# The columns of a group stored half by half: every TensorE read becomes one run of words

## The chip, the core and the metric

The kernel runs on one core of one Trainium2 chip. A core has TensorE (matrix products), VectorE (DVE), ScalarE (ACT), GpSimd (POOL), SyncE (SP, which issues the transfers), an on-chip memory SBUF of 128 partitions and a smaller memory PSUM into which TensorE writes. The metric is the device time of one execution in microseconds (us). Before the change the median of three runs is 1070.05 us (1069.75 to 1071.53).

## The reference

`x` has 128 batches, 64 heads and 1024 positions. Two layers are added onto it in turn.

```python
# layer 0: a base weight and a low-rank adapter, picked per batch by its id
y  = einsum('bsd,od->bso', x, W) + bias          # d = o = 1024
h  = einsum('bsd,brd->bsr', x, A[ids])           # rank 16
x1 = x + y + einsum('bsr,bor->bso', h, B[ids])
# layer 1: a causal convolution of each head with a filter K of 1024 taps
out = x1 + mask * (irfft(rfft(x1, 2048) * rfft(K, 2048))[..., :1024] + x1 * D)
```

K is a sum over 64 complex exponentials for each head, and mask cuts each batch at its own length.

## The kernel before, in words

All is computed in float32 by splitting: a number is the sum of a high part in the type fp32r and a low part, and a product of two numbers becomes three matmuls (high by high, low weights by high, high weights by low). ScalarE makes a high part by a copy (line 687), VectorE the low part by a subtraction (line 1105).

**First stage (to about 769 us).** The 128 batches are cut into 16 groups of 8. The data of a group are [128 positions, 8 tiles, 512 columns], where a column is one (head, batch) pair: 64 heads by 8 batches. The eight batches are two halves of four, so a head has eight words in a row: four of half 0, then four of half 1. The product of the 1024 by 1024 weight with the group is done by Strassen's scheme in Winograd's form: seven products of half-sized blocks in the place of eight, separately for the even output tiles (p = 0) and the odd ones (p = 1). A block holds the columns of one half only. So the moving operand of such a matmul is 256 columns in 64 runs of 4 words, 8 words apart. `block` (line 300) and `half` (line 304) cut these views. Four sums T1 to T4 of blocks are made by VectorE (lines 1209 to 1226); T1 to T3 are stored with the slot between head and batch. Their high part `t_hi` has two slots, so its runs of 4 words lie 8 words apart; their low part `t_lo` has three, so its runs lie 12 words apart. T4 is kept in the place of `x_lo`; its high and low parts go to `t_hi` and `t_lo` like the others.

`product_hi` (line 1810) runs 16 matmuls over a high moving part, high and low weights in turn; `product_lo` (line 1816) runs 8 over a low moving part with the high weights. `adapters_down` (line 1738) computes h with 32 matmuls a group, `adapters_up` (line 1782) adds the adapters' product; both read halves. Each matmul loads its own 128 by 128 weights first. The even tiles of group 0 alone are computed without the scheme, from all 512 columns at once (line 1748), with their adapters on line 1774.

TensorE's order is written out by hand: for each group and for both p the products P1, then `adapters_down`, P2, P6, the adapters of block 11, P3, P7, block 12, then P5, P4, blocks 22 and 21. Between them ScalarE copies one PSUM bank onto another (`seed_b`, `seed_c`, `seed_e`, on line 687), and ScalarE and VectorE carry results to `x1_sb` (lines 690 and 1262), which is laid out by head, tile and batch. From there they go to a scratch tensor in DRAM.

**Second stage (from about 769 us).** Head by head, 30 products on line 1970 of 384 or 512 columns, and two rotations of a state on line 2005 with 128 columns. Its moving operands of 512 columns are one run of words each.

The weights of five products stream from DRAM again for each group, on the transfer queue of SyncE, 1 MB each.

Of the kernel before, what the change touches and what calls it, by code (L numbers as in the profile page):

```python
# [5 lines left out]
F32 = mybir.dt.float32  # L6
F32R = mybir.dt.float32r
# [6 lines left out]
P = 128  # L14
# [13 lines left out]
def lora_s4d_kernel(nc, x_t, ids, lengths, w_even, w_odd, bias_t, lora_a, lora_b, log_dt, c_re, c_im,  # L28
# [5 lines left out]
    batch = ids.shape[1]  # L34
    G = batch // n_groups
    GH = G // 2
    heads = log_dt.shape[1]
# [19 lines left out]
    HALF = NT // 2  # L57
    QT = NT // 4
    NH = N // 2
# [11 lines left out]
    def place(name, shape, dt, at=None):  # L71
        size = 1 if dt is U8 else 2 if dt is BF16 else 4
        for n in shape[1:]:
            size *= n
        where = cursor[0] if at is None else at
        if at is None:
            cursor[0] = (where + size + 63) // 64 * 64
        assert where + size <= nc.sbuf_usable_end, (name, where + size)
        return nc.alloc_sbuf_tensor_at(name, shape, dt, offset=where)
# [80 lines left out]


    t_at = cursor[0]
    t_lo = place("t_lo", [P, HALF, heads, 3, GH], F32R)
    t_raw = place("t_raw", [P, HALF, heads, 3, GH], F32, at=t_at)
    t_hi_at = cursor[0]
    t_hi = place("t_hi", [P, HALF, heads, 2, GH], F32R)
    t4_raw = place("t4_raw", [P, NT, N], F32, at=x_lo_at)
    v_shape = [P, HALF, QT, P]
    s1_even = place("s1_even", v_shape, F32, at=zb_at)
# [3 lines left out]
    LO_SLOT = {"T1": 2, "T2": 0, "T3": 1, "T4": 0}  # L173
    HI_SLOT = {"T1": 0, "T2": 0, "T3": 1, "T4": 1}

    x1_at = cursor[0]
    x1_sb = place("x1_sb", [P, 2, heads, HALF, G], F32)
# [47 lines left out]
    acc = nc.alloc_psum_tensor("acc", [P, 8, BANK], F32)  # L225
# [47 lines left out]
    c_thi = {n: sem("c_hi_" + n) for n in T_NAMES}  # L273
    c_tlo = {n: sem("c_lo_" + n) for n in T_NAMES}
# [19 lines left out]
    def r32(ap):  # L294

        return ap.bitcast(F32)
# [2 lines left out]

    def block(t, r, c):  # L300

        return t[:, r * HALF:(r + 1) * HALF, :].rearrange("p k (h a b) -> p k h a b", a=2, b=GH)[:, :, :, c, :]

    def half(t, c):
        return t.rearrange("p (h a b) -> p h a b", a=2, b=GH)[:, :, c, :]

    def tile_of(p, r, i):

# [7 lines left out]
        return a_st[:, :, c, part, :].rearrange("p t (g r) -> p g t r", r=rank)  # L316

    def t_source(g, n):
        return block(t4_raw, 0, 1) if n == "T4" else t_raw[:, :, :, LO_SLOT[n], :]

    def bank_part(bank, i):
        return acc[:, bank, i * NH:(i + 1) * NH]

    def by_row(ap):
        return ap.rearrange("p (h b) -> p h b", b=GH)
# [13 lines left out]
    def plain_bank(i):  # L339
        return (TRIO[0] + (D_BANK,))[i]  # L340
# [80 lines left out]
    with nc.Block() as blk:  # L421
# [263 lines left out]
        def _(act):  # L685
            def copy(dst, src):
                return act.activation(dst, src, ACT.Copy)  # L687

            def biased(dst, src, tile):
                return act.activation(dst, src, ACT.Identity, bias=bias_sb[:, tile:tile + 1])  # L690
# [47 lines left out]
            def split_t(g, n):  # L738

                act.wait_ge(c_t[n], g + 1)  # L740
                if n == "T1":
                    act.wait_ge(m_p6[1], g + 1)
                elif n == "T4":
                    act.wait_ge(m_p7[1], g + 1)
                elif g > 0:
                    act.wait_ge(m_p5[1] if n == "T2" else m_p4[1], g)
                if g == 0 and n == "T2":
                    act.wait_ge(st_pad, 16)
                copy(t_hi[:, :, :, HI_SLOT[n], :], t_source(g, n)).then_inc(c_thi[n], 1)

            def split_a(g):
                act.wait_ge(ld_a, 16 * G * (g + 1))
# [50 lines left out]
            def even_out(i):  # L803

                act.wait_ge(m_even, i + 1)
                if i == 0:
                    act.wait_ge(c_blo, 2)
                    act.wait_ge(ld_bias, 16)
                biased(x1_sb[:, 0, :, i, :], acc[:, plain_bank(i), :].rearrange("p (h b) -> p h b", b=G),
                       2 * i).then_inc(c_even, 1)  # L810

            def out_11(p, g):
# [143 lines left out]
            split_v(S2)  # L956
            seed_b(1, 0)
            split_t(0, "T2")
            even_out(2)
            even_out(3)  # L960
            split_v(S4)
# [133 lines left out]
        def _(dve):  # L1095
# [8 lines left out]
            def minus_hi(dst, src, hi):  # L1104
                return dve.tensor_tensor(dst, src, r32(hi), ALU.subtract)  # L1105
# [97 lines left out]
            def x_block(r, c):  # L1203
                return block(x_raw, r, c)

            def t1(g):
                if g > 0:
                    dve.wait_ge(m_p5[1], g)
                dve.tensor_tensor(t_source(g, "T1"), x_block(0, 1), x_block(0, 0), ALU.subtract).then_inc(c_t["T1"], 1)

            def t3(g):
                if g > 0:
                    dve.wait_ge(m_p7[1], g)
                dve.tensor_tensor(t_source(g, "T3"), x_block(1, 1), x_block(0, 1), ALU.subtract).then_inc(c_t["T3"], 1)
# [12 lines left out]

            def split_t(g, n):
                dve.wait_ge(c_thi[n], g + 1)
                minus_hi(t_lo[:, :, :, LO_SLOT[n], :], t_source(g, n),  # L1230
                         t_hi[:, :, :, HI_SLOT[n], :]).then_inc(c_tlo[n], 1)

            def split_a(g):
                for c in range(2):
# [71 lines left out]
            k = {n: t[:, :] for n, t in tiny.items()}  # L1306
# [71 lines left out]
            def filter_weights():  # L1378
                lo_half, hi_half = slice(0, n_state), slice(n_state, P)

                mul("t1", "cre", "qr")
                mul("t2", "cim", "qi")
                link(dve.tensor_tensor(k["ctr"], k["t1"], k["t2"], ALU.subtract))
                mul("t1", "cre", "qi")
                mul("t2", "cim", "qr")
                link(dve.tensor_tensor(k["cti"], k["t1"], k["t2"], ALU.add))

                for o, half, src, by in (("p_cos", lo_half, "ctr", 2.0), ("p_cos", hi_half, "cti", -2.0),
                                         ("p_sin", lo_half, "cti", -2.0), ("p_sin", hi_half, "ctr", -2.0),
                                         ("q_cos", lo_half, "cti", -2.0), ("q_cos", hi_half, "ctr", -2.0),  # L1390
                                         ("q_sin", lo_half, "ctr", -2.0), ("q_sin", hi_half, "cti", 2.0)):
                    link(dve.tensor_scalar(tiny[o][half, :], tiny[src][half, :], by, None, ALU.mult))
# [333 lines left out]
        def _(pe):  # L1726
# [59 lines left out]
            def weights(p, g, j):  # L1786

                if p == 1:
                    if g == 0:
                        pe.wait_ge(c_vlo, v_order.index(j) + 1)  # L1790
                    return v_hi[:, j, :, :, :], v_lo[:, j, :, :, :]
                if j in KEPT:
                    if g == 1:
                        pe.wait_ge(c_elo, EVEN_ORDER.index(j) + 1)
                    slot = KEPT[j]
                else:
                    n = stream_of(g, j)
                    if 2 <= n < 4:
                        pe.wait_ge(c_elo, EVEN_ORDER.index(j) + 1)
                    elif n >= 4:  # L1800
                        pe.wait_ge(ld_ws[n % 2], stream_loads(n))
                    slot = n % 2
                return w_pair[:, slot, 0, :, :, :], w_pair[:, slot, 1, :, :, :]

            def product_hi(bank, w_hi, w_lo, hi, opens):

                for i in range(QT):
                    for k in range(HALF):
                        for s, w in enumerate((w_hi, w_lo)):
                            pe.matmul(by_row(bank_part(bank, i)), w[:, k, i, :], hi[:, k, :, :],  # L1810
                                      start=opens and i == 0 and k == 0 and s == 0, stop=False, skip_group_check=True)

            def product_lo(bank, w_hi, lo):
                for i in range(QT):
                    for k in range(HALF):
                        mm = pe.matmul(by_row(bank_part(bank, i)), w_hi[:, k, i, :], lo[:, k, :, :],  # L1816
                                       start=False, stop=False, skip_group_check=True)
                return mm

            def x_product(p, g, j, bank, r, c, opens):  # L1820
                w_hi, w_lo = weights(p, g, j)
                product_hi(bank, w_hi, w_lo, block(x_hi, r, c), opens)
                return product_lo(bank, w_hi, block(x_lo, r, c))

            def t_product(p, g, j, bank, n, opens):
                w_hi, w_lo = weights(p, g, j)
                pe.wait_ge(c_thi[n], g + 1)
                product_hi(bank, w_hi, w_lo, t_hi[:, :, :, HI_SLOT[n], :], opens)
                pe.wait_ge(c_tlo[n], g + 1)
                return product_lo(bank, w_hi, t_lo[:, :, :, LO_SLOT[n], :])  # L1830

            def p1(p, g):
                n = turns(p, g)
# [278 lines left out]
```

## Time and profile before

| what | value |
|---|---|
| median of three runs | 1070.05 us |
| the profiled execution | 1069.73 us |
| its span, first to last instruction | 1068.0 us |
| TensorE busy | 1061.2 us, 99% |
| VectorE busy | 848.5 us, 79% |
| ScalarE busy | 717.0 us, 67% |
| transfers | 284.62 MB, mean 266 GB/s |
| granted TensorE clock | 1.000 |

The median is 0.32 us above the profiled execution, and 1.73 us of that execution lie outside the span. The duration of one matmul in the profile is from its start to its modelled end, and successive matmuls overlap; the pace at which they follow each other is read from their starts, or from the busy time of a run of them.

### The profile page before, as it was taken

The numbers are of one execution on the slowest core, as the hardware profiler recorded it, in microseconds if no ns is written. First come the engines' busy times: TensorE is split into PE (matmuls) and PEld (weight loads), VectorE is DVE, ScalarE is ACT, GpSimd is POOL, SyncE is SP. The second block draws the span as 40 slices with busy tenths as digits, with TensorE's granted clock in tenths as the row PEclk, the third lists the DMA queues.
The fourth block names the chain that finished last, engine by engine and source line by source line (L and its number), as shares of the span: only waits on it lengthen the run. The fifth ranks groups of instructions, "written<-read, shape, count | busy, mean of one in ns | idle before, by whom it ended". The sixth has DMA issues, their size and how long they took to land.

```text
span 1068.0 us, 21568 instructions
## 1 busy us (share of the span) xinstructions
PE 1061.2 (99%) x8088; PEld 1028.8 (96%) x8088; DVE 848.5 (79%) x1263; ACT 717.0 (67%) x1260; POOL 28.6 (3%) x79
## 2 busy tenths in 40 slices
PE   9999999999999999999999999999999999999998
PEld 7999999999999999999999999999989999999997
DVE  7899887878698787878778787877488888888886
ACT  5755545755747466556557467465598888888885
POOL 0000000000000000000000000000010000000000
PEclk9999999999999999999999999999999999999999
DMA  8586758688786978868785888858798978798873
GB/s 290 202 304 221 275 191 284 199 300 307 226 269 211 298 225 277 282 229 275 229 308 179 296 260 259 293 194 283 264 346 286 350 287 335 294 326 317 304 263 123
DMA packets 162586, 284.62 MB, mean 266 GB/s; under 512 B 10739, under 2 KB 125620, under 8 KB 149044
## 3 DMA queue, kind: packets, MB, share of 16 engines
q1 hardware_dynamic: 162484, 283.26, 77.1%
q8 instruction: 64, 1.05, 0.4%
q14 instruction: 38, 0.31, 0.1%
HBM read 193.96 MB, written 89.26 MB: 265 GB/s over the span
## 4 chain that ended last, share of the span: by engine, by line
PE 97%; DVE 1%; ACT 1%; DMA 0%; issue 0%; DVEq 0%; SPq 0%; ACTq 0%
PE acc L1810 37%; PE acc L1970 25%; PE acc L1816 18%; PE acc L1738 5%; PE acc L1782 5%; PE acc L2005 3%; PE acc L1748 2%; DMA x_raw<-x_t 0%; PE acc L1915 0%; ACT x_hi L687 0%; PE acc L1774 0%; DVE x_sb L1262 0%; ACT L845 0%; ACT L851 0%; DVE g_sb L1460 0%
## 5 line engine op out<-in xcount | busy, mean ns | idle before, releaser
L1970 PE MATMUL acc<-u_hi,f_hi 128*128 128x512 f32 (+1 forms) x320 | 128.9, 403 | 0.0
L687 ACT ACTIVATE acc<-acc 128x512 f32<-128x512 f32 x93 | 54.0, 581 | 109.4 <-PE acc L1816 109.3
L1810 PE MATMUL acc<-t_hi,v_lo 128*128 128x256 f32 x512 | 123.0, 279 | 0.0
L1810 PE MATMUL acc<-t_hi,v_hi 128*128 128x256 f32 x512 | 122.9, 279 | 0.0
L1810 PE MATMUL acc<-t_hi,w_pair 128*128 128x256 f32 x960 | 122.4, 279 | 0.0
L1970 PE MATMUL acc<-u_lo,f_hi 128*128 128x512 f32 (+1 forms) x320 | 118.4, 370 | 0.0
L1970 PE MATMUL acc<-u_hi,f_lo 128*128 128x512 f32 (+1 forms) x320 | 118.2, 369 | 0.0
L1810 PEld LDWEIGHTS acc<-t_hi,w_pair 128*128 128x128 f32 x960 | 116.9, 188 | 0.0
L687 ACT ACTIVATE t_hi<-t_raw 128x1024 fp32r<-128x1024 f32 x64 | 67.9, 1061 | 61.7 <-DVE t_raw L1220 33.0
L1105 DVE TENSOR_TENSOR t_lo<-t_raw,t_hi 128x1024 fp32r<-128x1024 f32 x64 | 78.3, 1223 | 34.3 <-ACT t_hi L687 33.9
L1810 PEld LDWEIGHTS acc<-t_hi,v_lo 128*128 128x128 f32 x512 | 96.2, 188 | 0.0
L1810 PEld LDWEIGHTS acc<-t_hi,v_hi 128*128 128x128 f32 x512 | 96.2, 188 | 0.0
L1810 PE MATMUL acc<-x_hi,v_hi 128*128 128x256 f32 x384 | 92.6, 280 | 0.6 <-ACT acc L687 0.6
L1810 PE MATMUL acc<-x_hi,w_pair 128*128 128x256 f32 x720 | 92.9, 281 | 0.0
L1810 PE MATMUL acc<-x_hi,v_lo 128*128 128x256 f32 x384 | 92.3, 279 | 0.0
L1810 PEld LDWEIGHTS acc<-x_hi,w_pair 128*128 128x128 f32 x720 | 87.7, 188 | 0.9 <-issue 0.4
L1660 DVE COPY_PREDICATED out_sb<-mask,acc 128x1024 f32<-128x1024 uint8 (+1 forms) x65 | 84.5, 1301 | 2.4 <-PE acc L1970 2.4
L1262 DVE SCALAR_TENSOR_TENSOR x_sb<-acc,bias_sb,x_sb 128x256 f32<-128x256 f32 x124 | 53.9, 476 | 37.7 <-ACT x_sb L687 36.2
L690 ACT ACTIVATE x_sb<-acc,bias_sb 128x256 f32<-128x256 f32 (+1 forms) x128 | 54.4, 480 | 43.8 <-PE acc L1782 42.4
L1105 DVE TENSOR_TENSOR s_lo<-s_raw,s_hi 128x256 fp32r<-128x256 f32 (+1 forms) x128 | 44.7, 350 | 48.1 <-ACT s_hi L687 48.0
L1105 DVE TENSOR_TENSOR x_lo<-x_raw,x_hi 128x512 fp32r<-128x512 f32 x128 | 79.9, 684 | 1.6 <-ACT x_hi L687 1.1
L1105 DVE TENSOR_TENSOR u_lo<-u_raw,u_hi 128x1024 fp32r<-128x1024 f32 (+1 forms) x64 | 77.5, 1210 | 1.3 <-ACT u_hi L687 1.3
(205 smaller groups left out, 2673.3 us busy)
## 6 DMA issues: line engine op xcount, KB each, us to landing
w_pair<-weight_scratch SPq DMA_DIRECT2D x71, 1024.0 KB, 6.5
x_scratch<-x_sb SPq DMA_DIRECT2D x32, 1024.0 KB, 6.0
out<-out_sb SPq DMA_DIRECT2D x63, 512.0 KB, 4.8
x_raw<-x_t SPq DMA_DIRECT2D x15, 2048.0 KB, 11.1
u_raw<-x_scratch SPq DMA_DIRECT2D x14, 2048.0 KB, 11.8
wq_raw<-state_scratch SPq DMA_DIRECT2D x16, 1024.0 KB, 8.1
a_raw<-lora_a SPq DMA_DIRECT2D x128, 64.0 KB, 5.7
b_raw<-lora_b SPq DMA_DIRECT2D x128, 64.0 KB, 2.1
```

The lines of the kernel that those rows point to most:

```text
L687: return act.activation(dst, src, ACT.Copy)
L690: return act.activation(dst, src, ACT.Identity, bias=bias_sb[:, tile:tile + 1])
L1105: return dve.tensor_tensor(dst, src, r32(hi), ALU.subtract)
L1262: return dve.scalar_tensor_tensor(out=part_out(p, r, i, 1), in0=by_row(bank_part(bank, i)), scalar=bias_sb[:, tile:tile + 1], in1=part_out ...
L1660: return dve.copy_predicated(out_sb[h % OUT_BUFS][:, pars, :, :].rearrange("p k g n -> p (k g n)"), mask[:, pars, :, :, :].rearrange("p k ...
L1738: mm = pe.matmul(half(acc[:, H_BANK, :], c), a_st[:, t, c, :, :].rearrange("p k r -> p (k r)"), half(m[:, t, :], c), start=t == 0 and i == ...
L1748: mm = pe.matmul(acc[:, plain_bank(i), :], w, m, start=k == 0 and s == 0, stop=False)
L1782: mm = pe.matmul(by_row(bank_part(bank, i)), b_st[:, c, tile_of(p, r, i), :], half(m[:, :], c), start=False, stop=s == 1, skip_group_check ...
L1810: pe.matmul(by_row(bank_part(bank, i)), w[:, k, i, :], hi[:, k, :, :], start=opens and i == 0 and k == 0 and s == 0, stop=False, skip_grou ...
L1816: mm = pe.matmul(by_row(bank_part(bank, i)), w_hi[:, k, i, :], lo[:, k, :, :], start=False, stop=False, skip_group_check=True)
L1970: mm = pe.matmul(bank, w, m, start=first and i == 0, stop=last and i == 2, skip_group_check=onto_closed)
L2005: pe.matmul(state_cols(h, i + 1), rot[h % 2][:, :, :].rearrange("p k n -> p (k n)"), s_raw[h % 2][:, :, i, :], start=False, stop=True, ski ...
```

## The change

The column order inside a group becomes half, head, batch: first the 256 columns of half 0, then those of half 1. The host writes `x_t` in that order; it holds the same bytes and is loaded by the same transfers. `block` and `half` become slices of 256 consecutive columns. The sums are stored slot by slot, so `t_raw`, `t_hi` and `t_lo` hold a sum as 256 consecutive words for each tile. The outputs of lines 1738 and 1774 into PSUM, which were written in runs of four words, become one run too. `x1_sb` and all after it keep their layout; the one output that reads all 512 columns (`even_out`, group 0) gets a view that puts the halves back beside each other. The number, the kinds and the order of the instructions on every engine stay as they were, and no semaphore or wait is changed.

```diff
-    t_lo = place("t_lo", [P, HALF, heads, 3, GH], F32R)
-    t_raw = place("t_raw", [P, HALF, heads, 3, GH], F32, at=t_at)
+    t_lo = place("t_lo", [P, 3, HALF, NH], F32R)
+    t_raw = place("t_raw", [P, 3, HALF, NH], F32, at=t_at)
-    t_hi = place("t_hi", [P, HALF, heads, 2, GH], F32R)
+    t_hi = place("t_hi", [P, 2, HALF, NH], F32R)
...
-        return t[:, r * HALF:(r + 1) * HALF, :].rearrange("p k (h a b) -> p k h a b", a=2, b=GH)[:, :, :, c, :]
+        return t[:, r * HALF:(r + 1) * HALF, c * NH:(c + 1) * NH].rearrange("p k (h b) -> p k h b", b=GH)
 
     def half(t, c):
-        return t.rearrange("p (h a b) -> p h a b", a=2, b=GH)[:, :, c, :]
+        return t[:, c * NH:(c + 1) * NH].rearrange("p (h b) -> p h b", b=GH)
...
+    def t_part(t, slot):
+        return t[:, slot, :, :].rearrange("p k (h b) -> p k h b", b=GH)
...
-                copy(t_hi[:, :, :, HI_SLOT[n], :], t_source(g, n)).then_inc(c_thi[n], 1)
+                copy(t_part(t_hi, HI_SLOT[n]), t_source(g, n)).then_inc(c_thi[n], 1)
...
-                biased(x1_sb[:, 0, :, i, :], acc[:, plain_bank(i), :].rearrange("p (h b) -> p h b", b=G),
+                biased(x1_sb[:, 0, :, i, :].rearrange("p h (a b) -> p a h b", b=GH),
+                       acc[:, plain_bank(i), :].rearrange("p (a h b) -> p a h b", a=2, b=GH),
                        2 * i).then_inc(c_even, 1)
...
-                minus_hi(t_lo[:, :, :, LO_SLOT[n], :], t_source(g, n),
-                         t_hi[:, :, :, HI_SLOT[n], :]).then_inc(c_tlo[n], 1)
+                minus_hi(t_part(t_lo, LO_SLOT[n]), t_source(g, n), t_part(t_hi, HI_SLOT[n])).then_inc(c_tlo[n], 1)
...
-                product_hi(bank, w_hi, w_lo, t_hi[:, :, :, HI_SLOT[n], :], opens)
+                product_hi(bank, w_hi, w_lo, t_part(t_hi, HI_SLOT[n]), opens)
                 pe.wait_ge(c_tlo[n], g + 1)
-                return product_lo(bank, w_hi, t_lo[:, :, :, LO_SLOT[n], :])
+                return product_lo(bank, w_hi, t_part(t_lo, LO_SLOT[n]))
...
-        "x_t": xs.transpose(0, 4, 3, 2, 1).reshape(batch // g, P, -1),
+        "x_t": xs.reshape(batch // g, 2, g // 2, heads, nt, P).transpose(0, 5, 4, 1, 3, 2).reshape(batch // g, P, -1),
```

## Rows read from the trace of the kernel before

**Rows 1.** The page: busy time by engine, and TensorE's granted clock.
```profile
PE 1061.2 (99%) x8088; PEld 1028.8 (96%) x8088; DVE 848.5 (79%) x1263; ACT 717.0 (67%) x1260; POOL 28.6 (3%) x79
...
PEclk9999999999999999999999999999999999999999
```

**Rows 2.** TensorE's waits: line, who released it, total us, times, longest.
```profile
PE acc L1896 <- DVE rot L1109: 1.5, 1, 1.5
PE acc L1748 <- DVE x_lo L1105: 1.0, 1, 1.0
PE acc L1810 <- ACT acc L687: 0.6, 2, 0.4
```

**Rows 3.** Stretches: us, busy time (count) by engine, clock, DMA share, GB/s.
```profile
62.00:755.00 693.00, 692.56 (x5986) 690.25 (x5985) 544.83 (x850) 411.98 (x664) 1.71 (x2) 1.00 0.77 256
```

**Rows 4.** Groups by form, TensorE: count, then busy us, mean ns, idle before.
```profile
L1810 PE MATMUL acc<-t_hi,v_lo 128*128 128x256 f32 x512 | 123.0, 279 | 0.0
...
L1810 PE MATMUL acc<-t_hi,w_pair 128*128 128x256 f32 x960 | 122.4, 279 | 0.0
L1810 PE MATMUL acc<-x_hi,w_pair 128*128 128x256 f32 x720 | 92.9, 281 | 0.0
...
L1810 PE MATMUL acc<-x_hi,v_lo 128*128 128x256 f32 x384 | 92.3, 279 | 0.0
...
L1816 PE MATMUL acc<-t_lo,v_hi 128*128 128x256 f32 x512 | 69.7, 278 | 0.0
L1816 PE MATMUL acc<-t_lo,w_pair 128*128 128x256 f32 x480 | 65.3, 278 | 0.0
...
L1782 PE MATMUL acc<-hl,b_st 128*128 128x256 f32 x248 | 61.0, 279 | 0.0
...
L1738 PE MATMUL acc<-x_hi,a_st 128*128 128x256 f32 x256 | 60.7, 280 | 0.0
L1816 PE MATMUL acc<-x_lo,v_hi 128*128 128x256 f32 x384 | 52.8, 279 | 0.0
L1816 PE MATMUL acc<-x_lo,w_pair 128*128 128x256 f32 x360 | 49.5, 279 | 0.0
```

**Rows 5.** TensorE in order of time, group 0: start us, us, what.
```profile
20.04 0.39 PE L1748 MATMUL acc<-x_lo,w_pair 128*128 128x512 f32 x1
...
21.40 0.39 PE L1748 MATMUL acc<-x_lo,w_pair 128*128 128x512 f32 x1
```

**Rows 6.** TensorE in order of time, second stage, 384 columns.
```profile
901.32 0.34 PE L1970 MATMUL acc<-u_lo,f_hi 128*128 128x384 f32 x1
...
902.20 0.39 PE L1970 MATMUL acc<-u_hi,f_hi 128*128 128x512 f32 x1
```

**Rows 7.** TensorE's weight loads in order of time, behind two rotations.
```profile
901.04 0.19 PEld L1970 LDWEIGHTS acc<-u_hi,f_hi 128*128 128x128 f32 x1
901.15 0.19 PEld L1970 LDWEIGHTS acc<-u_lo,f_hi 128*128 128x128 f32 x1
```

**Rows 8.** Groups by form, ScalarE and VectorE.
```profile
L687 ACT ACTIVATE t_hi<-t_raw 128x1024 fp32r<-128x1024 f32 x64 | 67.9, 1061 | 61.7 <-DVE t_raw L1220 33.0 <-PE acc L1816 28.4
L687 ACT ACTIVATE v_hi<-v_raw 128x1024 fp32r<-128x1024 f32 x7 | 7.3, 1058 | 0.0
L690 ACT ACTIVATE x_sb<-acc,bias_sb 128x256 f32<-128x256 f32 x124 | 51.8, 473 | 42.4 <-PE acc L1782 42.4
L690 ACT ACTIVATE x_sb<-acc,bias_sb 128x512 f32<-128x512 f32 x4 | 2.5, 685 | 1.4 <-PE acc L1774 1.4
...
L1105 DVE TENSOR_TENSOR t_lo<-t_raw,t_hi 128x1024 fp32r<-128x1024 f32 x64 | 78.3, 1223 | 34.3 <-ACT t_hi L687 33.9
L1105 DVE TENSOR_TENSOR u_lo<-u_raw,u_hi 128x1024 fp32r<-128x1024 f32 x56 | 68.2, 1219 | 0.0
L1209 DVE TENSOR_TENSOR t_raw<-x_raw 128x1024 f32<-128x1024 f32 x16 | 19.6, 1224 | 0.5
```

More of the change, by code:

```diff
@@ L318, in t_source @@
     def t_source(g, n):
-        return block(t4_raw, 0, 1) if n == "T4" else t_raw[:, :, :, LO_SLOT[n], :]
+        return block(t4_raw, 0, 1) if n == "T4" else t_part(t_raw, LO_SLOT[n])
+    def t_part(t, slot):
+        return t[:, slot, :, :].rearrange("p k (h b) -> p k h b", b=GH)
     def bank_part(bank, i):
```

## The prediction, on record before the run

> **What bounds the kernel now.** I read the page first, for busy time and clock: TensorE is busy 1061.2 us of 1068.0 at the full granted clock in every slice; the next engine, VectorE, has 848.5 us [rows 1]. Then TensorE's waits: all of them together are 3.1 us, two of which (0.6 us) are in the first stage's products and the rest at the start [rows 2]. Then the stretches: in the sixteen-group part, 62 to 755 us, TensorE is busy 692.56 of 693.00 us while VectorE has 544.83 and ScalarE 411.98 [rows 3]. So the first stage is a queue of matmuls of 256 columns with no gap, and its time is their number times the pace at which they follow each other. Only a changed pace can change the time by much; what VectorE and ScalarE gain or lose lies beside TensorE, until it makes them late.
>
> The mean duration, 279 ns, is not that pace, since matmuls overlap. The pace comes from the busy time of a group: a run of n matmuls in a row is busy for (n-1) paces and one duration. For `product_lo`, in runs of 8 [rows 4]:
> - `x_lo` by `v_hi`: 384 matmuls are 48 runs, 52.8/48 = 1.100 us each; less 0.279 and divided by 7 that is 117.3 ns. `x_lo` by `w_pair`: 45 runs in 49.5 us, again 117.3 ns.
> - `t_lo` by `v_hi`: 64 runs in 69.7 us, 1.089 us each, 115.9 ns. `t_lo` by `w_pair`: 60 runs in 65.3 us, 115.8 ns.
> For `product_hi`, `t_hi` by `w_pair` in runs of 16: 60 runs in 122.4 us, (2.040-0.279)/15 = 117.4 ns. Where high and low weights have names of their own, a name's run spans 14 paces and a duration: `t_hi` by `v_lo`, (123.0/64-0.279)/14 = 117.3 ns; `x_hi` by `v_lo`, (92.3/48-0.279)/14 = 117.4 ns. `x_hi` by `a_st`, 16 runs in which it stands at every second of 32: (60.7/16-0.280)/30 = 117.1 ns.
>
> 256 columns at 2.4 GHz, the higher of the clock's two levels, are 106.7 ns. So each matmul carries 9 to 11 ns beyond its columns, and the question is whether the form of the read makes part of it.
>
> **The change part by part.**
>
> *The moving reads.* Affected are 6232 of the 8088 matmuls. From the counts [rows 4], with the partners of each row that have the same count: 1984 over `t_hi`, 1488 over `x_hi` and 744 over `x_lo` in the products, 992 over `t_lo`, 496 on line 1782, 512 on line 1738, 16 on line 1774. All but those over `t_lo` read runs of 4 words that lie 8 words apart (5240); `t_lo` reads runs of 4 words 12 words apart (992). The second stage and line 1748 read as before.
>
> Four groups at four different places in SBUF with runs 8 words apart have one pace, 117.1 to 117.4. The only group with another spacing has 115.8 to 115.9, with the same weights, the same line and the same PSUM views as `x_lo`. That is the nearest thing in this trace to an experiment on the form of a read: the form is worth 1.4 ns. It suggests that reads that come back at every second 4-word piece pay a little, and that reads which come to odd and even pieces alike do not. An unbroken run goes over odd and even pieces in turn, as the 12-word spacing does. My value for the new pace is therefore that of `t_lo`, 115.9 ns, for all. Gain: 5240 x 1.4 ns = 7.3 us; the 992 over `t_lo` stay. The rounding of the busy times moves this difference by up to 0.3 ns, or 1.6 us.
>
> Bounds from both sides. Below: a matmul needs its own weights, and the trace shows two weight loads following each other after 901.15-901.04 = 0.11 us behind the short rotations [rows 7]. At 110 ns for all, the gain is 5240 x 7.3 + 992 x 5.9 = 38.3+5.9 = 44 us. Above: unbroken reads exist in this trace, but with more columns. In group 0 six matmuls of 512 columns take 21.40-20.04 = 1.36 us, 226.7 ns each [rows 5], 13.4 above their 213.3. In the second stage five of 384 columns take 0.88 us, 176 ns, 16 above 160 [rows 6]. If 13.4 ns were a fixed price of any unbroken read, 256 columns would take 120.1 ns: 5240 x 2.8 + 992 x 4.2 = 14.7+4.2 = 18.9 us more. I take neither end: the value nearest in columns, line and weights is that of `t_lo`.
>
> The Trainium skill, "SBUF — State Buffer", section "Door 1: The DMA port swizzle", says that SBUF has lines of 16 bytes, that accesses within a line go at full speed, and that for fp32 four words can thus be had free. By it a run of 4 words is a whole line, the old reads cost what the new ones do, and the time would stay at 1069.7 us; the 1.4 ns between two spacings of whole lines speaks against taking it as exact.
>
> *The PSUM outputs* of lines 1738 and 1774 (528 matmuls) become unbroken. `x_hi` by `a_st` writes runs of 4 words at 117.1 ns, the matmuls over `t_hi` write one run at 117.3 to 117.4 [rows 4]. So 0, and at most 528 x 0.3 = 0.2 us either way. The Trainium skill, "Advanced Engine Details and Errata", section "PSUM Cachelines", has it that any broken pattern in PSUM slows matmuls much; this trace does not agree, 117.1 against 117.4 ns, and by the rule I would have had to add a gain on these 528.
>
> *VectorE and ScalarE.* The sums and splits become unbroken. `t_hi` takes 1061 ns against 1058 for `v_hi`, which is an unbroken copy of the same size; `t_lo` 1223 against 1219 for `u_lo`; a sum `t_raw` 1224 [rows 8]. So each instruction changes by 5 ns at most, 12 in a group, 0.06 us, all beside TensorE, which has no wait on them to lose. Cost 0. `even_out` gets a fourth dimension, four times: 685 ns for 512 elements now, against 473 for 256 in 4-word runs, which is 0.83 ns for each further element [rows 8], the pace of the unbroken copies. If every one doubled in time, that would be 2.7 us on ScalarE in group 0, where TensorE has products of odd tiles to do (P1, P2, P6) before it needs all those banks. 0 again.
>
> *Transfers and order.* Same bytes, same queue, same waits. A faster TensorE asks for the streamed weights 0.46 us earlier in a group of some 46 us; the transfer engines are 77% busy there [rows 3]. 0.
>
> *What is late next.* TensorE's two waits for ScalarE's bank copies (0.6 us in all) show that at two places VectorE and ScalarE have no slack [rows 2]. There TensorE's gain of that group, 7.3/16 = 0.46 us, is given back: 2 x 0.46 = 0.9 us. Elsewhere VectorE has 148 us of idle time in 693 [rows 3].
>
> Sum, against the profiled execution: 1069.73 - 7.3 + 0.9 = 1063.3 us. The median of before is 0.3 higher; I say 1063.
>
> **The rivals.**
>
> *A. The form of the read costs nothing* (chance 0.25). The 1.4 ns of `t_lo` come from something else, such as its place in SBUF beside the weights' place. For: 4-word runs already have a lower surplus over their columns (9 to 11 ns) than unbroken reads have (13 to 16). Against: `t_hi` lies right behind `t_lo` and has the pace of `x_hi`. Time: 1069.7, within 0.5 us.
>
> *B. An unbroken read brings more than the 12-word spacing does* (0.15). The surplus would shrink on all 6232 until the weight loads at 110 ns bind. For: the surplus is partly made of breaks in the read. Against: the unbroken 512-column reads keep 13.4 ns. Half way is 22 us, 1048 us; the end is 1026 us.
>
> *C. Unbroken reads carry a fixed price of 13.4 ns* (0.17), the rival on the other side: 1069.7+18.9 = 1089 us at the full size, 1079 at half. Its place is every matmul of the first stage. It decides from the point where the new pace is above the mean of before, (5240 x 117.3 + 992 x 115.9)/6232 = 117.1 ns. For: both unbroken widths show such a surplus. Against: a read in pieces would have to be cheaper than one in a run, and the surplus is not one number, 13.4 and 16.
>
> That the change does not do what it says is a small rival inside A: the views are still written by head and batch, and if the matmul still carried them as 64 steps of 4 words, their addresses would be unbroken all the same.
>
> **How the numbers follow.** Forecast 0.43, A 0.25, B 0.15, C 0.17. A measurement of this kernel tells 0.2%, 2.1 us, from no change. That is 0.34 ns of pace, so faster holds nearly all of the forecast and B: 0.55 after 0.03 for a forecast that comes out too small; the same 0.27; slower 0.18 with a little of A. The forecast's own range is 1060 to 1067. The range for 8 in 10 takes in A, most of B to 1043 and the lower half of C to 1078.
>
> **What would show it.** Right: `x_lo` in runs of 8 at 115.9 ns, so its two groups at 52.3 and 49.1 us busy (48 and 45 runs of 7 x 0.1159 + 0.279), `t_hi` by `w_pair` near 121.0 us busy, `t_lo` unchanged at 69.7, and the second stage as long as before. A would show all groups as before. B would show `t_lo` faster than 115 ns. C would show `x_lo` and `t_lo` near 120 ns. The forecast is wrong if `x_lo` and `t_lo` no longer differ but meet at another value than 115.9, or if TensorE's waits grow beyond 4 us.

## The result, and the profile after

The changed kernel takes 1087.03 us (median of four runs, 1086.29 to 1087.89) against 1070.05: a ratio of 1.0154, 95% interval 1.0142 to 1.0166. It is slower by 17.0 us, where 1063 was forecast and 1078 was the upper end of the range. Rival C had given 1089. The profiled execution took 1086.79 us with a span of 1085.1, 17.1 more than before.

The page of the changed kernel, busy times and clock, to be read against [rows 1]:

```profile
PE 1079.2 (99%) x8088; PEld 1047.2 (97%) x8088; DVE 848.8 (78%) x1263; ACT 717.2 (66%) x1260; POOL 28.6 (3%) x79
...
PEclk9999999999999999999999999999999999999999
```

TensorE is busy 18.0 us longer with the same 8088 matmuls at the same clock; VectorE and ScalarE are where they were. TensorE's waits, against [rows 2]:

```profile
PE acc L1899 <- DVE rot L1113: 1.5, 1, 1.5
PE acc L1751 <- DVE x_lo L1109: 0.5, 1, 0.5
PE acc L1813 <- ACT acc L690: 0.2, 1, 0.2
```

They fell from 3.1 to 2.2 us. So the time is in the pace, the distance between the starts of successive matmuls. Groups by form, against [rows 4] (lines are three further down):

```profile
L1813 PE MATMUL acc<-t_hi,w_pair 128*128 128x256 f32 x960 | 125.0, 283 | 0.0
...
L1819 PE MATMUL acc<-t_lo,v_hi 128*128 128x256 f32 x512 | 71.9, 283 | 0.0
...
L1819 PE MATMUL acc<-x_lo,v_hi 128*128 128x256 f32 x384 | 53.9, 283 | 0.0
```

By the same working as before: `x_lo` (53.9/48-0.283)/7 = 120.0 ns (117.3 before), `t_lo` (71.9/64-0.283)/7 = 120.1 (115.9), `t_hi` (125.0/60-0.283)/15 = 120.0 (117.4). All forms of before have become one number. In the order of time, three matmuls of line 1785 show how even it is; each starts 0.12 us after the last:

```profile
382.39 0.28 PE L1785 MATMUL acc<-hh,b_st 128*128 128x256 f32 x1
382.51 0.28 PE L1785 MATMUL acc<-hl,b_st 128*128 128x256 f32 x1
382.63 0.28 PE L1785 MATMUL acc<-hh,b_st 128*128 128x256 f32 x1
```

The starts in the record itself are 120 ns apart, one after the other, for thousands of matmuls; before, nearly all lay between 112 and 123. Sum: 5240 x 2.7 + 992 x 4.2 = 14.1+4.2 = 18.3 us, less 0.9 of waits that went, 17.4 against a span that grew by 17.1. The second stage did not change: in both kernels its last 299 us hold 1595 matmuls.

### The profile page after: what moved, and what is told of

The parts are those of the page before. It is cut to its first block, busy times and chain, and to the rows that moved or that the text cites. A ratio compares the mean times of both kernels' runs of the same rounds, so it can differ in the third digit from the quotient of the medians.

```text
span 1085.1 us, 21568 instructions
## 1 busy us (share of the span) xinstructions
PE 1079.2 (99%) x8088; PEld 1047.2 (97%) x8088; DVE 848.8 (78%) x1263; ACT 717.2 (66%) x1260; POOL 28.6 (3%) x79
## 4 chain that ended last, share of the span: by engine, by line
PE 99%; DMA 1%; SPq 0%; ACT 0%; issue 0%; DVEq 0%; DVE 0%
PE acc L1813 39%; PE acc L1973 25%; PE acc L1819 19%; PE acc L1741 6%; PE acc L1785 5%; PE acc L2008 3%; PE acc L1751 2%; DMA x_raw<-x_t 1%; PE acc L1918 0%; PE acc L1777 0%; DVEq L424 0%; SPq L454 0%; DVE x_lo L1109 0%; ACT x_hi L690 0%; ACT acc L690 0%
## 5 line engine op out<-in xcount | busy, mean ns | idle before, releaser
L1813 PE MATMUL acc<-t_hi,v_hi 128*128 128x256 f32 x512 | 125.6, 283 | 0.0
L1813 PE MATMUL acc<-t_hi,v_lo 128*128 128x256 f32 x512 | 125.6, 283 | 0.0
L1813 PE MATMUL acc<-t_hi,w_pair 128*128 128x256 f32 x960 | 125.0, 283 | 0.0
L1813 PEld LDWEIGHTS acc<-t_hi,w_pair 128*128 128x128 f32 x960 | 119.5, 192 | 0.0
L1265 DVE SCALAR_TENSOR_TENSOR x_sb<-acc,bias_sb,x_sb 128x256 f32<-128x256 f32 x124 | 53.9, 476 | 41.6 <-ACT x_sb L690 39.9
## 6 DMA issues: line engine op xcount, KB each, us to landing
x_raw<-x_t SPq DMA_DIRECT2D x15, 2048.0 KB, 11.3
```

The source lines that it names most:

```text
L1265: return dve.scalar_tensor_tensor(out=part_out(p, r, i, 1), in0=by_row(bank_part(bank, i)), scalar=bias_sb[:, tile:tile + 1], in1=part_out ...
```

## The experiments

Twelve kernels ran. A pace is worked out as above from the groups. "Quiet stretch" means extra matmuls behind the last product of the kernel before, when the other engines have almost nothing left to do; they read `u_hi` as moving operand and `f_hi` as weights, in sets of 16 or 32, and their results go to a bank that nobody reads. Both tiles start at the same place within 512 bytes, as all of the kernel's weights and moving tiles of these products do; such starts are called in step below. A start is given in words of 4 bytes, counted within 512 bytes from there.

**1 and 2. Half of the change at a time.** In the first only the sums are stored unbroken, in the second only the x columns and the adapters' operands.

```diff
 # sums only, against before (input order and block/half untouched)
+    t_lo = place("t_lo", [P, 3, HALF, NH], F32R)
+    t_hi = place("t_hi", [P, 2, HALF, NH], F32R)
 # x only, against the changed kernel (sums back to head, slot, batch)
+    t_lo = place("t_lo", [P, HALF, heads, 3, GH], F32R)
+    t_hi = place("t_hi", [P, HALF, heads, 2, GH], F32R)
```

> Only the sums are stored unbroken (t_raw, t_lo, t_hi slot by slot); the x columns and the adapter reads keep their runs of 4 words. Theory U, each unbroken read of 256 columns costs exactly 120.0 ns (256 + 32 clock periods) whatever is beside it: the 2976 matmuls over t_hi and t_lo go to 120.0, the 3256 others stay at 117.3; 1984 x 2.6 + 992 x 4.1 = +9.2 us, about 1079.3 us. Rival S, the time came with the input order or the transfers of x_t and not with the reads: no change, 1070 us. Rival M, mixed reads disturb each other and the others change too: x_lo no longer at 117.3.

> The x columns, the adapter reads and the two broken PSUM outputs are made unbroken; the sums keep head, slot, batch. Theory U: the 3256 matmuls over x_hi, x_lo, hh and hl go from 117.2 to 120.0 ns, +9 us, 1079 us, and t_lo stays at 115.9. With the sums-only kernel the two parts add to the 17 us of the whole change. Rival S: all 17 us are here, 1087 us.

Measured: sums only 1080.75 us, ratio 1.0101 (1.0084 to 1.0117); x only 1077.34, ratio 1.0063 (1.0046 to 1.0080). The parts are 10.4 and 7.0 us, together 17.4 for 17.0; 9 us were expected of the second. The groups of the sums-only kernel and then of the x-only kernel:

```profile
L1818 PE MATMUL acc<-t_lo,v_hi 128*128 128x256 f32 x512 | 71.9, 283 | 0.0
...
L1818 PE MATMUL acc<-x_lo,v_hi 128*128 128x256 f32 x384 | 52.9, 279 | 0.0
```

```profile
L1819 PE MATMUL acc<-t_lo,v_hi 128*128 128x256 f32 x512 | 69.8, 278 | 0.0
L1819 PE MATMUL acc<-x_lo,v_hi 128*128 128x256 f32 x384 | 53.9, 283 | 0.0
```

In the first, `t_lo` is at 120.1 and `x_lo` at 117.6; in the second `x_lo` at 120.0 and `t_lo` at 116.1. What is unbroken is at 120, and what is broken stays within 0.3 ns in these groups. On line 1740 the broken reads went from 117.1 to 117.8, so rival M has a small share. Theory U holds so far, S is out: the paces of the reads account for the time, and neither the input order nor its transfers are needed for it.

**3. Forms of the read in a quiet stretch.** 26 sets of 16, such as

```diff
+            for i in range(16):
+                pe.matmul(o(256), w(i), m(0, [[8, 64], [1, 4]]), start=i == 0, stop=i == 15, ...)
```

> The kernel before with 26 sets of 16 extra matmuls behind its last product, while the other engines are nearly idle; each set reads its moving operand in another form (run length and pitch in words) or has other sizes. Their results go to a PSUM bank that nobody reads. Theory U, a form's own price: unbroken 256 at 120 ns, runs of 4 with pitch 8 at 117, with pitch 12 at 116, also when all else is quiet; unbroken 512 at 226.7, 192 at 93.3, 128 at 66.7 if the 32 periods are per matmul. Rival L, the 32 periods come from the weight load: 64 weight columns in the place of 128 make the unbroken read cheaper. Rival D, the broken reads are only cheaper because the traffic of other engines shifts them: in the quiet stretch all forms have the same pace. Time: 416 matmuls of some 117 ns and a few longer, +50 us, 1120 us.

Measured 1124.33 us. TensorE in order of time; each row is a set: start, us, what, count.

```profile
1078.05 2.08 PE L2094 MATMUL acc<-u_hi,f_hi 128*128 128x256 f32 x16
1079.97 3.79 PE L2096 MATMUL acc<-u_hi,f_hi 128*128 128x256 f32 x16
1083.58 3.81 PE L2098 MATMUL acc<-u_hi,f_hi 128*128 128x256 f32 x16
1087.21 3.91 PE L2100 MATMUL acc<-u_hi,f_hi 128*128 128x256 f32 x16
...
1096.68 1.99 PE L2108 MATMUL acc<-u_hi,f_hi 128*64 128x256 f32 x16
1098.50 2.03 PE L2110 MATMUL acc<-u_hi,f_hi 128*64 128x256 f32 x16
```

L2094 is two runs of 128 words: (1079.97-1078.05)/16 = 120 ns. L2096 has runs of 2 words, every second pair: 3.61/16 = 226 ns; L2098 single words, every second: 227; L2100 every fourth: 233. So runs of 2 words and of 1 take nearly double, and 4-word runs are the shortest cheap form of those that ran (runs of 3 did not). The Trainium skill, "SBUF — State Buffer", section "Door 1: The DMA port swizzle", has lines of 16 bytes and asks for two hits in each; the runs of 2 words have two hits of the four and are doubled all the same, so this trace does not agree that two are enough. L2108, unbroken with 64 weight columns in the place of 128, has 1.82/16 = 114 ns. That is theory L: the price of the unbroken read came down with the weight load. Theory U failed in two more ways: an unbroken read that began at word 4 had starts 114 and 119 ns apart in turn, not 120, and unbroken reads of 128 and 192 columns settled near 112 ns in place of its 66.7 and 93.3. That last number is also the nearest thing to the prediction's lower bound of 110 ns for a matmul that loads its own weights. Theory D is out: pitch 12 had 115.8 ns (mean of 15 steps between starts) with nothing else running.

**4. Starts of the read in a quiet stretch.** 23 sets of 32.

> The kernel before with 23 sets of 32 extra matmuls behind its last product (results unread): unbroken reads that start at words 0 to 128 of the tile, with 64 and 96 weight columns, broken forms at other starts, and one set with the same weights every time. Theory P, the weight load's read and the moving read get in each other's way when they walk in step: the pace of an unbroken read depends on its start against the weights' start (120 at word 0, 117 or less from word 4), and is lower with fewer weight columns. Rival U, a fixed price of 32 clock periods for an unbroken read: 120 at every start and for 128 weight columns. About +85 us, 1155 us.

Measured 1152.19 us:

```profile
1071.02 3.89 PE L2084 MATMUL acc<-u_hi,f_hi 128*128 128x256 f32 x32
...
1078.53 3.79 PE L2088 MATMUL acc<-u_hi,f_hi 128*128 128x256 f32 x32
1082.16 4.00 PE L2090 MATMUL acc<-u_hi,f_hi 128*128 128x256 f32 x32
...
1101.24 3.99 PE L2100 MATMUL acc<-u_hi,f_hi 128*128 128x256 f32 x32
1105.07 3.80 PE L2102 MATMUL acc<-u_hi,f_hi 128*64 128x256 f32 x32
```

All are unbroken reads of 256 columns. From word 8 (L2084): (3.89-0.279)/31 = 116.5 ns. From word 16 (L2088): (1082.16-1078.53)/32 = 113.4. From word 24: 4.00 us of busy time, 120. From word 128, 512 bytes on (L2100): 3.83/32 = 119.7, as from word 0. With 64 weight columns: 113.7. The pace changes with the start of the read, over a range of 6.6 ns. Theory P holds, U fails. But P had said 117 or less from word 4 on, and there it was 119.0; of all the starts that ran here only words 8 and 16 are below 117.8, so being out of step is not enough. The set with the same weights every time has 120.0, as in step with changing ones. The broken reads move too: pitch 8 has 117.7 from word 0, 116.7 from word 4 and 119.9 from word 8.

**5. The changed kernel with shifted tiles.**

```diff
+    cursor[0] += 32
     x_hi_at = cursor[0]
 # and the same ahead of x_lo, t_lo, t_hi, hh and hl
```

> The changed kernel with x_hi, x_lo, t_lo, t_hi, hh and hl each moved on by 32 bytes (8 words) against the weights; nothing else differs. Theory P: the pace of the 6232 reads leaves 120.0, for 117 about -18 us, 1069 us. Rival U: 1087 us as without the shift.

The expectation misdescribes its kernel: the shifts add up, so that within 512 bytes x_hi stands 8 words on, x_lo 24, t_lo 40 and t_hi 56, and the adapters' weights moved too. Measured 1074.60 us, ratio 1.0048 (1.0031 to 1.0065): 12.4 of the 17.0 us came back though every read is unbroken (1069 was expected). `x_lo`, at word 24, is the dear one as in the quiet stretch:

```profile
L1825 PE MATMUL acc<-t_lo,v_hi 128*128 128x256 f32 x512 | 70.7, 280 | 0.0
...
L1825 PE MATMUL acc<-x_lo,v_hi 128*128 128x256 f32 x384 | 53.6, 281 | 0.0
```

`x_lo` 119.4 ns, `t_lo` 117.8.

**6 and 7. A clean shift of 16 words, with the new and with the old reads.**

```diff
+    cursor[0] += 64
     x_hi_at = cursor[0]
 ...
+    cursor[0] += 448          # a_st and b_st back in step with the other weights
     a_st = place("a_st", [P, NT, 2, 2, R2], F32R)
 ...
+    cursor[0] += 64
     hh = place("hh", [P, N], F32R)
```

> The changed kernel with x_hi, x_lo, t_lo, t_hi, hh and hl all moved by 64 bytes (16 words) against all weights, counted within 512 bytes (a_st and b_st stay in step with the other weights). Theory P, the start of the moving read against the weights' start sets the pace: 113.4 ns, as the unbroken read from word 16 in the quiet stretch, for all 6232: 6232 x 6.7 ns = 42 us less than the changed kernel, 1045 us, and 25 us less than before. Rival Q, the offset only breaks the lock and any start but 0 gives 117: 1069 us. Rival U: 1087 us.

> The kernel before (runs of 4 words) with the same shift of 64 bytes. Theory P holds for broken reads too: pace changes, pitch 12 from 115.9 to 116.7 as in the quiet stretch, pitch 8 by an unknown amount within 116 to 120: 1064 to 1085 us. Rival B, the broken read is indifferent to its start: 1070 us. If it stays well above 1045 us, breaking the read is worse than an unbroken read at the right start.

Measured: new reads 1071.02 us, ratio 1.0003 (0.9994 to 1.0013); old reads 1079.06, ratio 1.0072 (1.0056 to 1.0089). The first: 16 us gone by moving tiles 64 bytes, with a pace of (52.6/48-0.278)/7 = 116.8 for `x_lo` instead of 113.4: the miss is 3.4 ns, and rival Q's number. But 116.8 is a mean of two paces. TensorE in order of time, two runs of 16 of the same form:

```profile
104.33 2.05 PE L1816 MATMUL acc<-x_hi,w_pair 128*128 128x256 f32 x16
...
173.98 1.98 PE L1816 MATMUL acc<-x_hi,w_pair 128*128 128x256 f32 x16
```

Of the 217 runs of 16 on line 1816, read from start to start, 151 have 117.8 ns and 52 have 113.3; the 14 others hold longer steps, and none lies between. One start has two steady paces here, in one execution.

The second: the runs with pitch 8 became dearer, `x_lo` (53.5/48-0.281)/7 = 119.1 and `t_hi` 118.9, while `t_lo` with pitch 12 stayed at 115.6. For pitch 12, 116.7 was expected. The broken read is not indifferent to its start either, and the trace of the kernel before shows that by itself. On line 1738 the 16 matmuls of half 1, which begin at word 4, come first, then the 16 of half 0, from word 0:

```profile
298.96 0.28 PE L1738 MATMUL acc<-x_hi,a_st 128*128 128x256 f32 x1
...
300.83 0.28 PE L1738 MATMUL acc<-x_hi,a_st 128*128 128x256 f32 x1
...
302.60 0.28 PE L1738 MATMUL acc<-x_lo,a_st 128*128 128x256 f32 x1
```

Without the step between the halves that is 116.7 ns and 117.8, the same in all 16 groups and within 0.1 ns of experiment 4. The 117.3 of the groups by form is a mean over two starts.

**8. Does a start have one pace?**

> The kernel before with 23 sets of 32 extra matmuls behind its last product (results unread). Starts 16, 80, 144 and 272 of an unbroken read of 256 columns, twice word 16 behind other sets, and starts 0, 8 and 16 for 384 and 512 columns. Theory P: word 16 gives 113.4 whatever ran before, word 144 (16+128) the same, and 512 columns from word 16 fall from 226.7 to about 220. Rival R, the pace is a matter of the phase that the set before leaves: word 16 at other values on its second time. About +95 us, 1165 us.

Measured 1173.01 us:

```profile
1068.48 3.93 PE L2082 MATMUL acc<-u_hi,f_hi 128*128 128x256 f32 x32
1072.25 3.90 PE L2084 MATMUL acc<-u_hi,f_hi 128*128 128x256 f32 x32
1075.98 3.93 PE L2086 MATMUL acc<-u_hi,f_hi 128*128 128x256 f32 x32
...
1102.42 3.82 PE L2100 MATMUL acc<-u_hi,f_hi 128*128 128x256 f32 x32
1106.08 7.43 PE L2102 MATMUL acc<-u_hi,f_hi 128*128 128x512 f32 x32
1113.35 7.50 PE L2104 MATMUL acc<-u_hi,f_hi 128*128 128x512 f32 x32
...
1128.16 5.73 PE L2108 MATMUL acc<-u_hi,f_hi 128*128 128x384 f32 x32
```

Word 16 (L2082, L2086): 3.77/32 = 117.8, twice, where experiment 4 gave 113.4 for the same read; words 80, 144 and 272 also 117.8. Word 8 again 116.6. Word 112 (L2100) 3.66/32 = 114.4, its last 26 steps between starts 113.3 on average. So rival R's point stands beside P: the start does not fix one pace. Experiments 4 and 8 differ in the set that ran ahead, but no run shows what picks the pace. With 512 columns word 0 has 7.27/32 = 227 ns and word 16 has 229: nothing to gain there. With 384 columns word 0 settles at steps of 173.3 ns (L2108), 13.3 above the 160 of its columns.

**9. Weights and moving tiles moved together.**

```diff
+    cursor[0] += 64
     w_at = cursor[0]
```

> The changed kernel with all of weights and moving tiles moved by 64 bytes together, so that they start in step as before the move. Theory P (the start of the moving read against the weights' start): 120.0 ns as in the changed kernel, 1087 us. Rival A, the start of the moving read alone counts: as with the 64-byte shift of the moving tiles, 1071 us.

Measured 1088.38 us, ratio 1.0169 (1.0154 to 1.0185). Against experiment 6, what differs in what TensorE reads is the weights' place, and the 16 us are back:

```profile
L1820 PE MATMUL acc<-t_lo,v_hi 128*128 128x256 f32 x512 | 71.9, 283 | 0.0
...
L1820 PE MATMUL acc<-x_lo,v_hi 128*128 128x256 f32 x384 | 53.9, 283 | 0.0
```

These are the changed kernel's numbers to the last digit. The start of the read against the weights' start counts, and rival A, its own address alone, is out.

**10. A shift of 112 words.** As 6, with 448 and 64 bytes exchanged.

> The changed kernel with the moving tiles moved by 448 bytes (112 words) against the weights. In the quiet stretch an unbroken read from word 112 settled at 113.3 ns. Theory P with one pace for a start: 6232 x 6.7 ns less than the changed kernel, 1045 us. Rival R, a start allows several steady paces and what came before picks one: between 1045 and 1075 us, with runs that differ by more than 1 us.

Measured 1063.17 us (five runs, 1060.27 to 1069.88), ratio 0.9950 (0.9920 to 0.9981): faster than both kernels, by 0.5% against the one before. The groups:

```profile
L1816 PE MATMUL acc<-t_hi,w_pair 128*128 128x256 f32 x960 | 119.2, 277 | 1.6 <-issue 1.6
...
L1822 PE MATMUL acc<-t_lo,v_hi 128*128 128x256 f32 x512 | 68.7, 277 | 0.0
...
L1822 PE MATMUL acc<-x_lo,v_hi 128*128 128x256 f32 x384 | 51.5, 277 | 0.0
```

`x_lo` 113.7 ns, `t_lo` 113.8, `t_hi` 114.0: 6.2 ns less than the changed kernel, 38.6 us over 6232. Rival Q is out with that. Run by run, 176 of the 217 runs of 16 have 113.3 ns and 24 have 117.8. Only 23.6 us show, since TensorE now overtakes what feeds it. Its largest wait, then TensorE in order of time at the longest of them, then the stretches ahead of it, behind it and after that (us, busy and count by engine, clock, DMA share, GB/s):

```profile
PE acc L1816 <- DMA w_pair<-weight_scratch: 5.4, 3, 2.0
```

```profile
593.48 0.28 PE L1788 MATMUL acc<-hl,b_st 128*128 128x256 f32 x1
595.77 2.75 PE L1816 MATMUL acc<-x_hi,w_pair 128*128 128x256 f32 x16 [2.02 <-DMA w_pair<-weight_scratch]
598.32 1.91 PE L1822 MATMUL acc<-x_lo,w_pair 128*128 128x256 f32 x8
```

```profile
590.00:593.50 3.50, 3.50 (x34) 3.50 (x32) 3.36 (x7) 1.20 (x3) 0.00 (x0) 1.00 1.09 373
596.00:600.20 4.20, 4.20 (x25) 4.20 (x25) 4.08 (x6) 0.00 (x0) 0.00 (x0) 0.61 0.96 407
```

TensorE waits 11.8 us in all, 5.4 of them for the streamed weights: in the stretch ahead the transfer engines are full (share 1.09, 373 GB/s). And behind the 2.02 us wait the granted clock is 0.61 for 4.2 us: eight matmuls over `x_lo` start within 600.03-598.32 = 1.71 us, 214 ns each, the lower of the two levels, which costs some 1.7 us more. Waits of 1.89 and 1.61 us in the same run (at 361 and 515 us) had a clock of 1.00 behind them. With 9.6 us of added waits that is 11.3. From start to start the whole comes out: 6200 steps of the first stage's 256-column matmuls save 37.5 us, the 32 others, beside the waits and at the lower clock, cost 11.8, and all other matmuls 2.1, which leaves 23.6.

**11. An exact shift of 8 words**, the six moving tiles alone.

> The changed kernel with all moving tiles exactly 32 bytes (8 words) from the weights' start, counted within 512 bytes. The quiet stretches gave 116.6 ns twice, in a pattern of five that does not depend on what came before. Theory P: 6232 x (120.1-116.6) = 22 us less than the changed kernel, 1065 us, 0.4% under the kernel before.

Measured 1071.96 us (11 runs), ratio 1.0016 (1.0006 to 1.0026). The pace came out near the expectation, `x_lo` (52.6/48-0.279)/7 = 116.7, `t_lo` 116.8, `t_hi` 116.8, but against 117.1 on average before that is a gain of only 1.9 us, and 1.9 us of waits for streamed weights stand against it. From start to start the profiled run gains 2.4 us on the kernel before by its pace, and loses 3.0 in nine long steps and 0.8 elsewhere. My 1065 had subtracted from the changed kernel without adding waits. A miss. That the pace brought these waits is not shown: experiment 7, which is slower, has 1.5 us of them, and experiment 9 has 0.6.

**12. The weights' start and the weights' width.** 21 sets of 32.

> The kernel before with 21 sets of 32 extra matmuls behind its last product (results unread): the start of the weights is moved as well as that of the moving read, and the number of weight columns is 128, 64 or 32. Theory P: read and weights both from word 16, or both from word 8, give 119.6 to 120 as both from word 0; weights from word 8 with the read from word 0 is not 120. Theory P also: with 32 weight columns all forms, broken or not, come down to one pace of about 113.3. Rival F, the broken form itself costs: runs of 4 stay dearer than the unbroken read at 32 weight columns. About +80 us.

Measured 1145.22 us. Each pace is the distance to the next start over 32:

```profile
1064.67 3.99 PE L2084 MATMUL acc<-u_hi,f_hi 128*128 128x256 f32 x32
1068.49 3.99 PE L2086 MATMUL acc<-u_hi,f_hi 128*128 128x256 f32 x32
1072.32 3.81 PE L2088 MATMUL acc<-u_hi,f_hi 128*128 128x256 f32 x32
1075.97 4.00 PE L2090 MATMUL acc<-u_hi,f_hi 128*128 128x256 f32 x32
1079.81 3.95 PE L2092 MATMUL acc<-u_hi,f_hi 128*128 128x256 f32 x32
...
1102.27 3.80 PE L2104 MATMUL acc<-u_hi,f_hi 128*32 128x256 f32 x32
...
1109.54 3.90 PE L2108 MATMUL acc<-u_hi,f_hi 128*32 128x256 f32 x32
1113.27 3.79 PE L2110 MATMUL acc<-u_hi,f_hi 128*32 128x256 f32 x32
1116.90 3.90 PE L2112 MATMUL acc<-u_hi,f_hi 128*64 128x256 f32 x32
```

Read and weights both from word 0 (L2084) 119.4, both from word 16 (L2086) 119.7, both from word 8 (L2090) 120.0; read from word 0 and weights from word 16 (L2088) 114.1, its steady steps 113.3. Theory P, in a stretch where almost nothing else runs. With 32 weight columns the unbroken read (L2104) has 113.8 and the one with pitch 12 (L2110) 113.4, but the one with pitch 8 (L2108) keeps 3.73/32 = 116.6. Here rival F is right for pitch 8 and theory P's second half wrong.

Three sets fit no simple rule of distance. The read from word 0 with the weights from word 120 has 117.8, though they lie apart as the read from word 8 and the weights from word 0, which have 116.8. That read from word 8 takes 118.9 with 64 weight columns, more than with 128. And pitch 8 with the weights 8 words on takes 120.0: that pace is not a mark of unbroken reads.

So the pace has two parts, in ns for 256 columns:

| form of the read | 32 weight columns | 128, in the kernel, tiles in step (broken: mean over its starts) | 128, lowest steady pace seen |
|---|---|---|---|
| unbroken | 113.4 to 113.8 | 120.0 | 113.3 |
| 4 words, pitch 12 | 113.4 | 115.9 | 113.3 |
| 4 words, pitch 8 | 116.6 | 117.3 | 116.7 |

## Why the prediction was wrong, point by point

**What bounds the kernel.** Right: TensorE's queue, its pace, nothing else. Its waits stayed at 2.2 us, and a changed pace was the whole result.

**The step that failed** is the one on the moving reads: "an unbroken run goes over odd and even pieces in turn, as the 12-word spacing does. My value for the new pace is therefore that of `t_lo`, 115.9 ns, for all." It measured 120.0, and not for `x_lo` alone: `t_lo`, which was to stay at 115.9, went there too. The form does cost what I saw in it: with a short weight load, pitch 8 is 3.2 ns dearer than pitch 12 or an unbroken read (experiment 12). What was missing is the second reader. Every matmul has a weight load beside it, itself an unbroken read, and all weights and moving tiles start at the same place within 512 bytes. An unbroken read in step with its weights is 6.7 ns dearer than the cheapest (120.0 against 113.3), a broken one in this kernel only 2.6 (pitch 12) or 0.7 (pitch 8). So on the 5240 the change took away 3.2 ns of form and 0.7 of step and brought 6.7 of step. That the two readers' reads of SBUF collide is an explanation that fits the starts, the weights' own start (experiment 9) and the weights' width (experiments 3, 4, 12); the place in the hardware where they meet no run shows, and the three sets at the end of experiment 12 are left unexplained by it. The prediction's rival A had named the place in SBUF beside the weights' place as a cause, but for the 1.4 ns alone, and took the effect of the change to be 0.

**The weight I gave to rows.** I had the number: 13.4 ns above the columns for unbroken reads of 512 [rows 5], which at 256 gives 120.1. I set it aside because 384 columns had 16, which was no steady pace (experiment 8 has 13.3 there, nearly the surplus of 512), and because `t_lo` shared line and weights with the changed reads. But `t_lo` shared everything save the property that was about to change, and the rows with that property were the 512-column ones. The 1.4 ns themselves were a difference of two means over several starts (words 0 and 4 for pitch 8; 0, 4 and 8 for pitch 12), and line 1738 held 1.1 ns between two starts of one form. Rival C's size was right (18.9 worked out, 17.0 measured); its reason was not: no fixed price belongs to an unbroken read, as the shifts of experiments 6 and 10 show.

**The Trainium skill.** By its 16-byte lines ("SBUF — State Buffer", section "Door 1: The DMA port swizzle") 4-word runs cost nothing. With pitch 12 and a short weight load that holds within 0.4 ns; with pitch 8 it is 3.2 ns off. A sentence I had not weighed speaks to the failed step: "TensorE: Matmul & The Clock Gate", section "Step-by-step: what each phase is for", says that the weight load has a read port of its own and takes nothing from the running matmul. Experiment 9 against 6, 1088.38 against 1071.02 us, does not agree with the second half; whether there are two ports no run shows.

**PSUM outputs** at no cost: right, lines 1741 and 1785 came to the same pace though only one of them had had a broken output. **VectorE and ScalarE** at no cost: right, 848.8 against 848.5 and 717.2 against 717.0 us. **Transfers** at no cost: right for this pace; experiment 10 shows where it ends. **What is late next**: never tested by the change itself, but at 113.8 ns the waits came, 5.4 us for streamed weights, which I had put at 0, against 1.3 for ScalarE.

## What to carry to other kernels

Where matmuls with a new weight each are back to back, lay out the weights and the moving tile by their starts against each other, not only by the form of the read: try two or three offsets of one of them, which costs no instruction. An unbroken read was the cheapest form at a few starts only (words 16 and 112 of those that ran), and one of the dearest in step with the weight load. When a change alters a property, price it from rows that have the new property, even at another size, before rows that are alike in all else.

## What the hardware showed that I had not expected

- 256 columns: 120.0 ns in step, 113.3 with the weights' start 16 words past the read's, which is the read from word 112 (one place within 512 bytes), 116.6 from word 8, and 113.4 or 117.8 from word 16. The form of the read is the same in all of them.
- The steady paces lock in: most unbroken sets in step settle on steps of 120 within some ten matmuls, the cheap ones on 113.3, and keep them. In experiment 6 runs of 16 keep either 113.3 or 117.8, with nothing between.
- Runs of 2 words, and single words two apart, take 226 to 227 ns for 256 columns, single words four apart 233.
- A wait of 2.02 us was followed by a granted clock of 0.61 over 4.2 us, a wait of 1.89 us in the same run was not (experiment 10).
- Open: the whole table of starts, and how to choose the cheap one of two steady paces; runs of experiment 10 differ by 9.6 us, those of the kernel before by 3. The two longest, 1068.07 and 1069.88 us, have a mean clock of 0.997 and 0.995, the others 0.998.
